# Two attention layers and a mixture of experts on one core: the projections of batches 1 and 2 placed earlier, experts' weights loaded after the output rows, routing and first constants in another order, 1 KB pieces in two writes

## The reference, cut to what matters

```
x = x + tanh(g0) * attention0(layernorm(x), ctx, mask)      # 16 heads of 16, masked
x = x + tanh(g1) * ffn0(layernorm(x))                       # 256 -> 768 -> 256, fake-quantized
x = x + tanh(g2) * attention1(layernorm(x), ctx)            # 16 heads of 16
x = x + tanh(g3) * moe1(layernorm(x))                       # 32 experts, top 1, 160 places each
```

## Time and profile before

| | us |
|---|---|
| median of 3 runs | 1417.95 (1414.85 to 1423.94) |
| the profiled execution's own time | 1419.35 |
| its span, first to last instruction | 1418.1 |
| PE busy / DVE / ACT / POOL | 1205.2 / 899.1 / 681.2 / 539.1 |

### The profile page before, as it was taken

How to read it: one execution, slowest core, us unless ns; L and a number is a source line. 1 busy time by engine, 2 the same in 40 slices (tenths; PEclk the granted TensorE clock), 3 DMA queues, 4 the chain that set the end, 5 groups by cost and what they waited for, 6 DMA issues and landing times.

```text
span 1418.1 us, 24478 instructions
## 1 busy us (share of the span) xinstructions
PE 1205.2 (85%) x8913; PEld 845.1 (60%) x8913; DVE 899.1 (63%) x2697; ACT 681.2 (48%) x1156; POOL 539.1 (38%) x815
## 2 busy tenths in 40 slices
PE   2699999999999699975949957888998989865998
PEld 2467777767776344332428835666666666545897
DVE  2568787787677555796886534666765766742333
ACT  1255655655655344653853314555655656541221
POOL 4344443454342000896001222433443544313555
PEclk8699999999999799997979978999999999986999
DMA  5555555455451410000014464665575564325983
GB/s 136 135 132 126 126 138 140 117 128 130 113 138 40 120 45 0 1 1 0 0 29 136 149 139 96 145 150 155 150 179 151 131 148 109 91 109 179 286 240 41
DMA packets 126035, 162.34 MB, mean 114 GB/s; under 512 B 10834, under 2 KB 114380, under 8 KB 119750
## 3 DMA queue, kind: packets, MB, share of 16 engines
q1 hardware_dynamic: 116272, 151.40, 41.4%
q0 software_dynamic: 7296, 8.15, 3.2%
q10 hardware_dynamic: 2346, 1.22, 0.4%
HBM read 108.75 MB, written 52.53 MB: 114 GB/s over the span
## 4 chain that ended last, share of the span: by engine, by line
PE 43%; DMA 9%; POOL 7%; DVE 6%; issue 5%; ACT 2%; SPq 1%; ACTq 0%; POOLq 0%; DVEq 0%
PE PS L547 9%; PE PS L587 5%; PE PS L560 5%; PE PS L301 5%; DMA QS<-NT 4%; PE PS L361 4%; PE PS L344 3%; PE PS L320 3%; DMA QS<-qd 2%; PE PS L596 2%; POOL UQ L1408 2%; PE PS L419 2%; DMA qd<-PP 2%; PE PS L308 2%; POOL bufd L1478 1%
## 5 line engine op out<-in xcount | busy, mean ns | idle before, releaser
L692 ACT ACTIVATE P<-PS 128x512 f32<-128x512 f32 x512 | 304.2, 602 | 206.8 <-PE PS L347 94.7
L931 DVE TENSOR_REDUCE NM<-PS 128x2 f32<-128x512 f32 x256 | 174.7, 687 | 138.1 <-PE PS L320 137.2
L320 PE MATMUL PS<-KS,QS 96*128 96x256 bf16 x1024 | 202.6, 280 | 59.9 <-DMA QS<-qd 41.0
L344 PE MATMUL PS<-QS,KS 99*128 99x256 bf16 x1024 | 228.3, 277 | 28.6 <-DMA QS<-NT 23.5
L928 DVE CUSTOM_DVE_ANT_0 MX<-PS,NQ 128x256 bf16<-128x256 f32 x512 | 193.6, 419 | 89.6 <-PE PS L320 87.8
L320 PEld LDWEIGHTS PS<-KS,QS 96*128 96x128 bf16 x1024 | 88.3, 99 | 129.0 <-DMA QS<-qd 44.2
L547 PE MATMUL PS<-XNT,wup 128*128 128x512 f16 x576 | 132.5, 392 | 10.6 <-DVE AM L1203 10.6
L344 PEld LDWEIGHTS PS<-QS,KS 99*128 99x128 bf16 x1024 | 97.5, 100 | 71.8 <-DMA QS<-NT 27.0
L361 PE MATMUL PS<-P,V 128*32 128x256 f32 x2048 | 138.7, 389 | 1.7 <-ACT P L692 1.7
L347 PE MATMUL PS<-NK,identb 128*128 128x256 bf16 x512 | 127.1, 273 | 0.0
L547 PEld LDWEIGHTS PS<-XNT,wup 128*128 128x128 f16 x576 | 57.1, 101 | 84.4 <-DVE AM L1203 14.1
(11 more groups left out here) (238 smaller groups left out, 2422.9 us busy)
## 6 DMA issues: line engine op xcount, KB each, us to landing
kd<-PP SPq DMA_DIRECT2D x32, 384.0 KB
KS<-kd SPq DMA_DIRECT2D x32, 384.0 KB, 4.5
qd<-PP SPq DMA_DIRECT2D x32, 384.0 KB
QS<-qd SPq DMA_DIRECT2D x32, 384.0 KB, 4.5
WH<-in_wex SPq DMA_DIRECT2D x16, 768.0 KB
KS<-kd SPq DMA_DIRECT2D x32, 256.0 KB, 5.2
QS<-qd SPq DMA_DIRECT2D x32, 256.0 KB, 5.4
WG<-in_wex SPq DMA_DIRECT2D x10, 768.0 KB
```

Source lines behind the costliest of these rows:

```text
L320: ins = tensor.matmul(PS[:, bk, 256 * qt:256 * qt + 256], t.QS[b % 3][0:96, h, 128 * qt:128 * qt + 128], t.KS[b % 3][0:96, h, :], start=Tr ...
L344: ins = tensor.matmul(o, t.KS[b % 3][0:99, h, 128 * kt:128 * kt + 128], t.QS[b % 3][0:99, h, :], start=True, stop=(L == 1))
L692: scalar.activation(t.P[h % 8][:, :, :], PS[:, h % 2, :].rearrange("p (k n) -> p k n", k=2), ACT.Exp).then_inc(s_ex, 1)
L931: ins = vector.tensor_reduce(nm[:, :, h], PS[:, bk, :].rearrange("p (t n) -> p t n", t=2), X, ALU.max, negate=True)
```

## The change

Six edits, none of which changes the amount of arithmetic.

1. **Heads earlier at the start.** `head_start(b)` gives the slot at which a batch's head begins, counted as 16s + k: -22 for batch 1 (slot (-2, 10)), -6 for batch 2 (slot (-1, 10)), 16(b-2) as before for the others. All five engines take their head work from it. Values follow 13 slots later: batch 1's in (-1, 7), batch 2's in (0, 7). In layer 1 the keys and transposed x of batch 1 thereby fall into the slots that are interleaved with the down projection, behind batch 12's.
2. **SP's loads split** into rows, ctx and mask. The first loads are x rows, mask, key weights, ctx, where they were key weights, rows, ctx, mask. In layer 1 the key weights are loaded with the others at (-3, 0).
3. **Experts' weights** at k = 15, behind the output rows, where they were at k = 11.
4. **Routing** on DVE and ACT one slot earlier (k = 7, 8, 9), `pe_ranks` at 13 for 12, the slot numbers at 14 and 15 for 13 and 14, the scatters of the first four groups one slot later.
5. **POOL's setup**: gate times bias moves to slot (-3, 4), the clearing of the value tiles behind slot (-2, 2); the wait for the constant row is gone from POOL.
6. **Writes of the parts** with `(p m)` for `(m p)`: a partition's two 512-byte pieces become one run of 1 KB in DRAM. The host permutes the rows of the query and key weights to match.

```diff
+def head_start(b):
+    return {1: -22, 2: -6}.get(b, 16 * (b - 2))
+
+def heads_at(s, k):
+    found = []
+    for b in range(max(s, 0), min(s + 4, NB)):
+        kk = 16 * s + k - head_start(b)
+        if 0 <= kk < 16:
+            found.append((b, kk))
+    return found
...
-            if 0 <= s + 2 < NB:
-                if k == 0:
-                    pe_keys(L, s + 2)
-                if k == 1:
-                    pe_xn(L, s + 2)
-                if k == 3:
-                    pe_queries(L, s + 2)
-                if k == 13:
-                    pe_values(L, s + 2)
+            for b, kk in heads_at(s, k):
+                if kk == 0:
+                    pe_keys(L, b)
+                if kk == 1:
+                    pe_xn(L, b)
+                if kk == 3:
+                    pe_queries(L, b)
+                if kk == 13:
+                    pe_values(L, b)
...
-                if L == 1 and k == 12 and GROUP_OF[s - 2][1] == GROUP_OF[s - 2][2] - 1:
+                if L == 1 and k == 13 and GROUP_OF[s - 2][1] == GROUP_OF[s - 2][2] - 1:
                     pe_ranks(GROUP_OF[s - 2][0])
...
-                at = 16 * (s - (b0 + nb + 1)) + k - 15
+                at = 16 * (s - (b0 + nb + 1)) + k - (16 if g < 4 else 15)
...
         def pool_program():
             pool_setup()
-            pool.wait_ge(d_cr, 16)
-            pool_values(0)
             for s, k in slots(0):
+                if (s, k) == (-3, 4):
+                    pool_biases()
                 pool_slot(0, s, k)
+                if (s, k) == (-2, 2):
+                    pool_values(0)
...
-            sync.dma_start(dd[b % 3].rearrange("s (m p) n -> p s m n", p=128), PP[1 - which][:, :, :, :]).then_inc(done, 16)
+            sync.dma_start(dd[b % 3].rearrange("s (p m) n -> p s m n", m=2), PP[1 - which][:, :, :, :]).then_inc(done, 16)
...
+            if L == 1 and (s, k) == (-2, 12):
+                sp_stack(L, 0, 0)
+                sp_stack(L, 0, 1)
+            for b, kk in heads_at(s, k):
+                held = L == 1 and b == 0
+                if kk == 3:
+                    sp_parts(L, b, 0)
+                if kk == 5 and not held:
+                    sp_stack(L, b, 0)
+                if kk == 6:
+                    sp_parts(L, b, 1)
+                if kk == 8 and not held:
+                    sp_stack(L, b, 1)
...
-                if L == 1 and k == 11 and s - 1 < 8:
-                    sp_expert_weights(s - 1)
...
                 if L == 1 and k == 15:
                     sp_base(s - 1)
+                    if s - 1 < 8:
+                        sp_expert_weights(s - 1)
```

More of the change, by code:

```diff
@@ L788, in act_slot @@
                 act_heads(L, s, 0)
-            if 0 <= s + 2 < NB:
-                if k == 0:
-                    act_split(L, s + 2, 0)
-                if k == 1:
-                    act_xt(L, s + 2)
-                if k == 3:
-                    act_split(L, s + 2, 1)
-                if k == 13:
-                    act_values(L, s + 2)
+            for b, kk in heads_at(s, k):
+                if kk == 0:
+                    act_split(L, b, 0)
+                if kk == 1:
+                    act_xt(L, b)
+                if kk == 3:
+                    act_split(L, b, 1)
+                if kk == 13:
+                    act_values(L, b)
             if 0 <= s - 1 < NB:
@@ L807, in act_slot @@
                     act_logits(s - 2)
-                if L == 1 and k == 8 and GROUP_OF[s - 2][1] == GROUP_OF[s - 2][2] - 1:
+                if L == 1 and k == 7 and GROUP_OF[s - 2][1] == GROUP_OF[s - 2][2] - 1:
                     act_route(GROUP_OF[s - 2][0])
@@ L1129, in dve_slot @@
                 dve_max(L, s + 1, k)
-            if 0 <= s + 2 < NB:
-                if k == 2:
-                    dve_mid(L, s + 2, 0)
-                if k == 5:
-                    dve_mid(L, s + 2, 1)
+            for b, kk in heads_at(s, k):
+                if kk == 2:
+                    dve_mid(L, b, 0)
+                if kk == 5:
+                    dve_mid(L, b, 1)
             if 0 <= s - 1 < NB:
@@ L1505, in pool_slot @@
                 pool_maxima(L, s + 1, 0)
-            if 0 <= s + 2 < NB:
-                if k in (0, 3):
-                    pool_rest(L, s + 2, int(k == 3))
-                if k in (2, 5):
-                    pool_low(L, s + 2, int(k == 5))
+            for b, kk in heads_at(s, k):
+                if kk in (0, 3):
+                    pool_rest(L, b, int(kk == 3))
+                if kk in (2, 5):
+                    pool_low(L, b, int(kk == 5))
             if 0 <= s + 3 < NB:
@@ L1562, in sp_weight, with sp_load_mask, sp_load_rows @@
             sync.dma_start(TL[L].W[n][:, :, :], a[f"w{n}{L}"].rearrange("(k p) n -> p k n", p=128)).then_inc(d_w[n], 16)
-        def sp_load(L, b):
-            n, t = L * NB + b, TL[L]
-            i, j = b % 5, b % 2
+        def sp_load_mask(b):
+            sp.wait_ge(s_pen, b - 1)
+            sp.wait_ge(s_av, b - 1)
+            sync.dma_start(t0.MM[b % 2][:, :, :], a["mm"][b]).then_inc(d_m[b % 2], 16)
+        def sp_load_rows(L, b):
+            n, t, i = L * NB + b, TL[L], b % 5
             if b >= 5:
@@ L1578, in sp_load, with sp_load_ctx @@
             sync.dma_start(t.XB[i][:, :, :], rows(a["x"] if L == 0 else x2d, b)).then_inc(d_x[i], 16)
+        def sp_load_ctx(L, b):
+            n, t, j = L * NB + b, TL[L], b % 2
             if b >= 2:
@@ L1653, in sp_slot @@
             if s == -3 and k == 0:
-                sp_load(L, 0)
+                sp_load_rows(L, 0)
+                if L == 0:
+                    sp_load_mask(0)
+                sp_weight(L, "k")
+                sp_load_ctx(L, 0)
                 for n in "qvo":
@@ L1657, in sp_slot @@
             if 0 < s + 3 < NB and k == 2:
-                sp_load(L, s + 3)
-            if 0 <= s + 2 < NB:
-                held = L == 1 and s == -2
-                if k == 3:
-                    sp_parts(L, s + 2, 0)
-                if k == (12 if held else 5):
-                    sp_stack(L, s + 2, 0)
-                if k == 6:
-                    sp_parts(L, s + 2, 1)
-                if k == (12 if held else 8):
-                    sp_stack(L, s + 2, 1)
+                sp_load_rows(L, s + 3)
+                sp_load_ctx(L, s + 3)
+                if L == 0:
+                    sp_load_mask(s + 3)
+            if L == 1 and (s, k) == (-2, 12):
+                sp_stack(L, 0, 0)
+                sp_stack(L, 0, 1)
+            for b, kk in heads_at(s, k):
+                held = L == 1 and b == 0
+                if kk == 3:
+                    sp_parts(L, b, 0)
[5 more added lines that the diff above has]
+                    sp_stack(L, b, 1)
             if 0 <= s - 1 < NB:
@@ L1736, in _inputs @@
     f = np.ascontiguousarray
-    order = np.arange(256).reshape(16, 16).T.reshape(-1)
+    order = np.arange(256).reshape(16, 16).T.reshape(128, 2).T.reshape(-1)
     out = {
```

18 lines of the change are left out of this document (7 added, 11 removed).

## The result

The changed kernel takes **1372.79 us**, median of 4 runs (1368.23 to 1374.43), beside 1416.40 (1410.88 to 1423.94) for the kernel before: a ratio of 0.968, 95% interval 0.963 to 0.974. The forecast was 1386, its range 1374 to 1403, so the time lies 13 us under the forecast and 1.2 us under the range. A second set of runs of the changed kernel, beside other experiments, gave 1377.30 (1373.14 to 1380.04, 6 runs) and a ratio of 0.972 (0.969 to 0.975). The first profiled execution took 1374.43 us, the longest of its four and the sixth shortest of all ten of both sets; its span (first to last instruction) is 1373.2 and its granted clock 0.945, where it was 0.932.

What follows compares the result with a forecast made beforehand. The prediction took PE to set the pace, busy for 1205.2 of 1418.1 us, with gains in its idle time and lower clock. Terms 8 + 7.5 + 12 + 5 + 1 = 33.5 off 1419.35 gave 1386 us, range 1374 to 1403.

Steps and rivals of the forecast that it cites:

- C: Layer 1's loaded batches: experts' weights behind the output rows free the maxima's DMA; 12 us, between 0 and 17.
- D: Routing in layer 1: waits for the count inside the layer go; 5 us, between 1 and 9.
- E: Writes of the parts in 1 KB pieces finish sooner where they are on the path; 1 us, between 0 and 4.
- B: Start of layer 1: later waits and batch 2's head go, less 2.5 and 3.5 in charges; 7.5 us, between 1 and 12.
- A: Start of layer 0: earlier setup and heads, less a stall of DVE; 8 us, between 3 and 12.
- Setup: Part of A: without POOL's wait for the constant row, layer 0's first scores come up to 4.2 us earlier; 4 taken.
- The stall of DVE: Charge in A: DVE waits for batch 2's late mask in layer 0, holding PE's scores too; 4.5 us, bounds 0 and 8.
- 1.6 us in two batches: 3: Part of C: the idle gap costs clock, 1.6 us of PE's busy time, counted in two batches; 3 us.
- The maxima's DMA is not freed: Rival: the read of queries alone holds that DMA, so C is 0; 1398 us, chance 0.13.
- the starts give nothing: Rival: batch 2's late loads lengthen DVE's wait and its queries' read is late again; 1401.5 us, chance 0.12.
- Slower: Rival: the weights push the keys' write, so PE waits for the queries' read in eight batches; 1429 us, chance 0.03.
- More than the sum: Rival: no charge for the stalls of A and B, and all of E; 1375 us, chance 0.08.

Runs made afterwards that it cites:

- heads_layer1: The changed kernel with the early heads in layer 1 only, layer 0 starting its batches as before: 1376.37 us, ratio 0.974.
- heads_layer0: The changed kernel with the early heads in layer 0 only, layer 1 starting its batches as before: 1382.37 us, ratio 0.978.
- weights_k11: The changed kernel with the experts' weights back at k = 11, ahead of the output rows: 1391.90 us, ratio 0.984.
- scatters_late: The changed kernel with the first three groups' scatters in later slots, none ahead of the keys' and queries' parts: 1373.06 us, ratio 0.970.
- pieces_512: The changed kernel with the two writes in 512-byte pieces again: 1379.64 us, ratio 0.974; repeated in the second set: 1382.38 us, ratio 0.975.
- heads_minus2: The changed kernel with the heads of batches 3 to 15 two slots earlier as well: 1383.62 us, ratio 0.976.

## Why the prediction was off

**The sum and the ledger.** The sum was taken from one execution of 1419.35 us; from the median of 1416.40 it would have said 1383, so the miss is one of the terms and not of the base. By the landmarks the prediction said 8 for layer 0, nothing for the feed-forward stage, 7.5 for the start of layer 1 and 18 for C, D and E in the rest of it: 33.5. Measured in the first profile: 7.4, 2.9 (11.9 less the 1.6 below and 7.4), 13.8 and 20.7: 44.8. The surplus of 11.3 has three parts: 6.3 at the start of layer 1, 2.7 in the rest of it, 2.9 in the stretch that varies by itself; layer 0 takes 0.6 back. The second set of runs, at 1377.3, lies inside the range. The steps that failed are B's charges (a stall of 3.5 us of which PE felt 0.65, and nothing for the first wait) and, in C, the price of the clock.

**A, 8 predicted, 7.4 measured at the end of layer 0.** Right in size, which is partly luck, as two wrong parts cancel. Setup: 4 predicted, 4.3 at the first scores, 5.4 at the first landmark and 4.6 at the end, each good to 2 or 3. The stall of DVE: 4.5 charged. It came at the place and for the reason given, but DVE waited 2.26 us and PE behind it 0.85, since its scores are buffered. Against that, heads_layer1 puts the early heads of layer 0 at 3.5 where my terms with the real stall give 7.7. Where the rest goes is open: PE waits 3.07 us for DVE at 72.26, but only 1.61 at that place in the second profile.

**B, 7.5 predicted, 13.8 measured at its place.** This step failed in its charges. The first wait fell from 11.09 to 8.15, 2.9 that I had at nothing. The down projection grew by 1.4 in this pair (70.7 to 72.1 from its start to the first values behind it); over all traces it takes 69.9 to 70.7 without early heads in layer 1 and 72.1 to 72.9 with them, so the charge of 2.5 was near. In this pair the two together are about 1.6. The other 12.2, in the table from the first landmark to the second batch, compare with 13.5 of gains (7.8 + 5.75) less 3.5 for the stall: DVE waited 2.6 us for batch 2's rows, and PE 0.65 behind it. A part of the 12.2 is clock, for which B had no term. The windows between these landmarks, in the kernel before and then in the changed one:

```profile
843.33:868.24 24.91, 19.83 (x122) 13.11 (x120) 12.41 (x27) 11.60 (x21) 8.87 (x18) 0.82 0.55 118
868.24:897.86 29.62, 24.29 (x184) 17.20 (x184) 15.08 (x34) 14.16 (x27) 8.88 (x18) 0.88 0.51 111
```

```profile
831.42:853.03 21.61, 17.50 (x116) 10.60 (x115) 12.96 (x26) 10.93 (x19) 8.58 (x18) 0.84 0.66 160
853.03:873.75 20.72, 19.77 (x176) 13.79 (x174) 14.70 (x33) 13.60 (x26) 8.90 (x18) 1.00 0.34 79
```

PE's busy time falls by 6.9 us (moved work and clock together, which no run separates) and its idle time by 5.3, where the sum had 7.8 of waits less the stall. heads_layer0 confirms the place with 12.0. By the end of attention the same pair of profiles leaves 7.5, and the second profile of the changed kernel 4.8, so the forecast of 7.5 for the whole is met and the surplus is at the start. Why later batches give some of it back is open.

**C, 12 predicted, 14.7 measured alone and 18.7 to 20.5 in the loaded batches of the changed kernel.** The mechanism is right: weights at k = 11 delay the maxima's DMA (7.58 us to land for 5.80), PE waits, and a read of queries issued just before does not. The waits were sized well, 9 against 8.5 to 11.2 of idle time. **The term that failed is the clock**: "1.6 us in two batches: 3". Six of the eight batches pay it, in the kernel before and again in weights_k11: 6.2 to 9.3. I had seen one window at 0.94 and one at 1.00 and counted from these, where one table of all the windows of layer 1 would have shown 0.94 in six of eight. With 6 x 1.6 the sum is 1379, inside the forecast's own bounds and 6.5 from the result (with the four that the move alone lifts it is 1382); my upper bound of 17 was too low for the same reason. Some of it is returned: in the first profile batches at 0.88 and 0.94 follow later, and over the whole attention layer C is worth 15.8 us.
The rule in the Trainium skill ("DMA: Bandwidth & Descriptors", Queues, rings and completion order) that an engine takes turns between queues packet by packet would have made C nothing. The runs with the weights at k = 11 and at k = 15 disagree with what I drew from it, that the small DMA waits for a packet or so: 12 KB on ACT's queue landed 1.8 and 1.1 us later (7.58 for 5.80, 7.09 for 6.00) with 768 KB more on SP's queue. The rule itself is not refuted by that, since no run shows how long a packet of the weights takes.

**D, 5 predicted, 5.1 to 5.4 measured.** The waits for the count fell by 7.9 where I had 5.5, as only one of the two of the tail stayed. The waits for the queries' read behind the groups stayed, as charged, and with them the loss of clock, which was not charged.

**E, 1 predicted; the write itself is faster, its worth in the kernel unsettled.** From the first write of keys to the issue of its read it is 2.54 us with 1 KB pieces and 2.76 with 512 B, and the profiles of each kind agree within 0.02, so the longer piece is worth 0.2 us there. In the kernel's time it is -1.8 to 5 us.
The figure of the Trainium skill ("DMA: Bandwidth & Descriptors", Specifications) that 512 B is the smallest piece at full rate would make it 0; the 2.76 against 2.54 of these writes speak against that by a little.

**Rivals.** "The maxima's DMA is not freed" and "the starts give nothing" fell with weights_k11 and the two runs on heads. "Slower" fell: the keys' write goes out at 886.69, 6.5 us behind the weights, and no loaded batch waits longer than 0.2 us for QS<-qd but the one behind the group's end. "More than the sum", 1375 at 0.08, was the nearest, for a part of the reason it gave: the stalls cost little. Its other part, all 4 us of E, is not shown, and the clock was not in it.

## What to carry to other kernels

An idle gap of PE in the middle of dense work can cost more than its length: in most batches with a gap of 3 us or more here the clock fell too, and that cost 1.6 us of busy time or more. Count such batches from a table of the windows of all of them, not from two. A stall of an engine behind a buffer costs the consumer only what the buffer does not hold, here 0.85 of 2.26 us. A profile of the same program varies by some microseconds in stretches that no edit touches, so landmarks common to both traces say more than the spans.

## What the runs showed of the hardware

- In the loaded batches of weights_k11 and in those behind the groups' ends the granted clock was 0.94 or 0.88 where PE had idled in one piece for 2.78 and 3.66 us (behind the groups' ends) or 3.53 and 3.04 us (with weights), and in two for 2.06 (changed kernel) and 2.07 us (scatters_late). A window at 0.94 spent part of its time at the 1.2 GHz level, those at 1.00 all of it at 2.4. With the gap filled by matmuls whose results nobody reads, eight of eight loaded batches stayed at 1.00.
- The length of the longest gap alone does not decide it. The first loaded batch of pieces_512, whose longest gap is 1.83 us, stands at 0.93, and one of the kernel before, with 3.03 us, at 1.00:

```profile
874.93:900.63 25.70, 23.87 (x194) 17.55 (x192) 17.04 (x42) 15.01 (x29) 10.06 (x19) 0.93 0.63 158
```

```profile
1058.73:1084.01 25.28, 22.25 (x194) 16.60 (x192) 17.05 (x42) 14.90 (x29) 10.02 (x19) 1.00 0.61 156
```

- Ten 128x256 f32 matmuls take about 4.2 us at a granted clock of 1.00, twice the estimate of 2.2.
- The first write of keys, 384 KB, in pieces of 1 KB was done 0.2 us sooner than in pieces of 512 B (2.54 for 2.76 us to the issue of the read that waits for it).
- The waits that one edit removes can be longer than the time it gives: heads_minus2 took 10.7 us of waits away and lost 8.7 us.
